# A graph layer with a mixture of experts on one core: the last loads of the expert outputs as two halves, their sums and stores in six pieces

## The reference

```python
xn = _layernorm(x, axis=-1)
x = x + _L0_gnn_ref(xn, edge_index, edge_attr_64, ...) + _L0_mix_ref(xn[None], ...)[0]
x = x + _L0_ffn_ref(_layernorm(x, axis=-1)[None], ...)[0]
...
    rw, re = jax.lax.top_k(probs, TOP_K)          # TOP_K = 2, weights made to sum to 1
    out = tokens
    for e in range(E):
        h = jax.nn.gelu(tokens @ w1[e] + b1[e], approximate=False)
        y = h @ w2[e] + b2[e]
        out = out + combine[:, e:e + 1] * y
```

## Time and profile before

| | us |
|---|---|
| median of 3 runs | 1223.35 (1216.89 to 1226.21) |
| profiled execution, own time | 1224.02 |
| profiled execution, span of the core | 1222.2 |
| last scatter of expert outputs issued (GpSimd) | 1181.99 |
| first load of the tail issued | 1184.14 |
| VectorE's last add ends | 1217.39 |

### The profile page before, as it was taken

How to read it: one execution, slowest core, us unless ns; L and a number is a source line. 1 busy time by engine, 2 the same in 40 slices (tenths; PEclk the granted TensorE clock), 3 DMA queues, 4 the chain that set the end, 5 groups by cost and what they waited for, 6 DMA issues and landing times.

```text
span 1222.2 us, 20643 instructions
## 1 busy us (share of the span) xinstructions
PE 943.8 (77%) x6706; PEld 678.6 (56%) x6707; DVE 677.0 (55%) x2018; ACT 357.3 (29%) x912; POOL 781.7 (64%) x575
## 2 busy tenths in 40 slices
PE   2308998798778999999999999925997008999960
PEld 2304544344336888888887888814886005666630
DVE  2306998677576666666566666305878402333324
ACT  0082232122113434434443444402434002222210
POOL 2588888888888888788888888860016771333320
PEclk9999999988898999999999999967979558999985
DMA  9944555545444565565555554467223232222239
GB/s 332 224 56 44 106 91 102 80 41 108 75 39 66 91 101 86 79 109 92 83 91 92 92 84 41 40 113 231 75 69 99 77 92 74 87 87 84 86 93 261
DMA packets 152487, 121.43 MB, mean 99 GB/s; under 512 B 123015, under 2 KB 142035, under 8 KB 148435
## 3 DMA queue, kind: packets, MB, share of 16 engines
q0 software_dynamic: 69376, 31.04, 24.8%
q1 hardware_dynamic: 76098, 75.82, 22.2%
q10 hardware_dynamic: 6926, 13.44, 3.5%
HBM read 75.23 MB, written 45.88 MB: 99 GB/s over the span
## 4 chain that ended last, share of the span: by engine, by line
PE 57%; POOL 17%; DMA 9%; issue 6%; DVE 5%; ACT 3%; SPq 1%; ACTq 0%; POOLq 0%; DVEq 0%
POOL edge_sums L636 14%; PE ps L1198 8%; PE ps L1043 7%; PE ps L1015 7%; PE ps L908 6%; PE ps L952 4%; PE ps L938 3%; PE ps L1024 3%; POOL routed_rows L659 3%; DMA edges<-in_edge_attr 3%; PE ps L1142 3%; DMA r2t<-expert_outputs 2%; PE ps L1199 2%; DMA edge_sums<-sums,addr 2%; PE ps L1047 2%
## 5 line engine op out<-in xcount | busy, mean ns | idle before, releaser
L636 POOL DMA_INDIRECT edge_sums<-sums,addr x416 | 648.0, 1558 | 159.9 <-issue 120.9
L908 PE MATMUL ps<-edges,same 128*128 128x65 f32 x832 | 121.2, 294 | 59.4 <-DMA edges<-in_edge_attr 36.2
L791 ACT ACTIVATE r<-ps 128x500 f32<-128x500 f32 (+1 forms) x225 | 126.2, 586 | 114.4 <-PE ps L1015 81.3
L908 PEld LDWEIGHTS ps<-edges,same 128*128 128x128 f32 x832 | 109.1, 206 | 79.9 <-DMA edges<-in_edge_attr 36.1
L1271 DVE SCALAR_TENSOR_TENSOR same<-srow,src_f,below 128x128 f32<-128x128 int32 x416 | 118.3, 346 | 39.2 <-DMA srow<-in_src_row 38.9
L667 POOL DMA_INDIRECT expert_outputs<-r x56 | 54.4, 972 | 120.9 <-DVE r L1648 118.3
L701 ACT ACTIVATE sums<-ps 128x260 f32<-128x260 f32 x104 | 40.7, 392 | 269.3 <-PE ps L908 172.0
L1198 PE MATMUL ps<-r2t,r 128*128 x448 | 117.6, 385 | 0.3 <-issue 0.3
L1381 DVE TENSOR_TENSOR r2t<-ps,r 125x2048 f32<-125x2048 f32 x50 | 113.1, 2262 | 0.0
L1015 PE MATMUL ps<-ident,r2t 125*128 125x125 f32 x800 | 105.8, 275 | 3.8 <-DVE r2t L1381 3.3
L1043 PE MATMUL ps<-r 128*64 128x125 f32 x1600 | 108.2, 277 | 0.0
(11 more groups left out here) (224 smaller groups left out, 1351.0 us busy)
## 6 DMA issues: line engine op xcount, KB each, us to landing
srow<-in_src_row SPq DMA_DIRECT2D x26, 1024.0 KB, 5.4
edges<-in_edge_attr SPq DMA_DIRECT2D x26, 512.0 KB
r<-routed_rows SPq DMA_DIRECT2D x56, 129.0 KB, 2.0
edge_sums<-sums,addr POOLq DMA_INDIRECT x416, 3.3
hpre_rows<-r ACTq DMA_DIRECT2D x25, 250.0 KB, 2.8
r<-hpre_rows SPq DMA_DIRECT2D x25, 250.0 KB, 2.7
edge_sums<-sums SPq DMA_DIRECT2D x4, 1040.0 KB, 14.6
r2t<-in_ew SPq DMA_DIRECT2D x4, 1024.0 KB, 14.6
```

The source lines that it names most:

```text
L636: pool.indirect_dma_start(out=tables[k], out_offset=bass.IndirectOffsetOnAxis(ap=addr[:, j:j + 1], axis=0), in_=sums[:, j % OR, :], in_off ...
L791: act.activation(phT[0:rows, j // 2 % 2 * 2 + j % 2, :], bank(1 + j % 2, rows, 0, QC * P), ACT.Copy).then_inc(grp_ready[j % 2], 1)
L908: m = mm(bank(b, 128, c0 + k * F, c0 + (k + 1) * F), lhsT=same[:, j % SR, :], rhs=edges[:, h, j % CH, :], start=True, stop=True)
```

## The change

Instead of five groups of 5 tiles, the loads come in two halves, of 13 tiles (into `r2t`) and 12 tiles (into `r1`, the large work buffer whose expert tiles are free by then). Each load now takes 13312 or 12288 bytes per partition in one run, and there are 8 load DMAs in place of 20. The sums and the stores are in six pieces of 5, 4, 4 tiles (first half) and 4, 4, 4 (second half). Pieces 0, 2, 4 are stored from SP, pieces 1, 3, 5 from ACT: 12 store DMAs in place of 10. The bytes loaded, added and stored are the same.

```diff
+        HALVES = ((0, 13), (13, T))
+        PIECES = ((0, 5), (5, 9), (9, 13), (13, 17), (17, 21), (21, T))
...
         def outputs_of(g):
-            if g < 2:
-                at_ = (srow[:, :, :].rearrange("p h c -> p (h c)").bitcast(fp32), sums[:, :, :].rearrange("p r f -> p (r f)"))[g]
-                return at_[0:P, 0:2 * FT * C].rearrange("p (a t c) -> p a t c", a=2, t=FT)
-            w = 2 * FT * C
-            return r2t[0:P, (g - 2) * w:(g - 1) * w].rearrange("p (a t c) -> p a t c", a=2, t=FT)
+            t0, t1 = HALVES[g]
+            at_ = (r2t, r1)[g][0:P, 0:2 * (t1 - t0) * C]
+            return at_.rearrange("p (a t c) -> p a t c", a=2, t=t1 - t0)
...
-            for g in range(T // FT):
+            for g, (t0, t1) in enumerate(HALVES):
                 for a, z in PARTS:
                     sp.dma_start(outputs_of(g)[a:z, 0, :, :], youts[0:N, :]
-                                 .rearrange("(p t) c -> p t c", p=P)[a:z, g * FT:(g + 1) * FT, :]).then_inc(yb_loaded[g], 16)
-            for g in range(0, T // FT, 2):
-                sp.wait_ge(yb_added, g + 1)
+                                 .rearrange("(p t) c -> p t c", p=P)[a:z, t0:t1, :]).then_inc(yb_loaded[g], 16)
+            for i, (t0, t1) in list(enumerate(PIECES))[0::2]:
+                sp.wait_ge(yb_added, i + 1)
                 for a, z in PARTS:
-                    sp.dma_start(out.rearrange("(p t) c -> p t c", p=P)[a:z, g * FT:(g + 1) * FT, :],
-                                 x_res[a:z, g * FT:(g + 1) * FT, :]).then_inc(stored, 16)
-            sp.wait_ge(stored, 32 * (T // FT))
+                    sp.dma_start(out.rearrange("(p t) c -> p t c", p=P)[a:z, t0:t1, :], x_res[a:z, t0:t1, :]).then_inc(stored, 16)
+            sp.wait_ge(stored, 32 * len(PIECES))
...
             v.wait_ge(res_ready, T)
-            for g in range(T // FT):
-                xv = x_res[:, g * FT:(g + 1) * FT, :]
+            for t0, t1 in PIECES:
+                g = t0 // HALVES[1][0]
+                lo = t0 - HALVES[g][0]
+                xv = x_res[:, t0:t1, :]
                 v.wait_ge(yb_loaded[g], 64)
-                link(v.tensor_tensor(xv, xv, outputs_of(g)[:, 0, :, :], ALU.add))
-                v.tensor_tensor(xv, xv, outputs_of(g)[:, 1, :, :], ALU.add).then_inc(yb_added, 1)
+                link(v.tensor_tensor(xv, xv, outputs_of(g)[:, 0, lo:lo + t1 - t0, :], ALU.add))
+                v.tensor_tensor(xv, xv, outputs_of(g)[:, 1, lo:lo + t1 - t0, :], ALU.add).then_inc(yb_added, 1)
```

More of the change, by code:

```diff
@@ L366, in gps_layer @@
         ys_stored = [sem(f"ys_stored{h}") for h in range(SB)]
-        yb_loaded = [sem(f"yb_loaded{g}") for g in range(T // FT)]
+        yb_loaded = [sem(f"yb_loaded{g}") for g in range(len(HALVES))]
         yb_added = sem("yb_added")
@@ L884, in _ @@
             act.wait_ge(ey_ps, NS)
-            for g in range(T // FT):
+            for g, (t0, t1) in enumerate(HALVES):
                 for a, z in PARTS:
                     act.dma_start(outputs_of(g)[a:z, 1, :, :], youts[N:2 * N, :]
-                                 .rearrange("(p t) c -> p t c", p=P)[a:z, g * FT:(g + 1) * FT, :]).then_inc(yb_loaded[g], 16)
-            for g in range(1, T // FT, 2):
-                act.wait_ge(yb_added, g + 1)
+                                  .rearrange("(p t) c -> p t c", p=P)[a:z, t0:t1, :]).then_inc(yb_loaded[g], 16)
+            for i, (t0, t1) in list(enumerate(PIECES))[1::2]:
+                act.wait_ge(yb_added, i + 1)
                 for a, z in PARTS:
-                    act.dma_start(out.rearrange("(p t) c -> p t c", p=P)[a:z, g * FT:(g + 1) * FT, :],
-                                 x_res[a:z, g * FT:(g + 1) * FT, :]).then_inc(stored, 16)
+                    act.dma_start(out.rearrange("(p t) c -> p t c", p=P)[a:z, t0:t1, :], x_res[a:z, t0:t1, :]).then_inc(stored, 16)
         @block.tensor
```

## The result

The changed kernel takes 1225.84 us in the median of 20 runs (1219.06 to 1232.02), the kernel before 1219.32 in 20 (1212.71 to 1227.88). The ratio is 1.0041 with a 95% interval of 1.0022 to 1.0061: 2.7 to 7.4 us slower, 5.0 in the middle. (The means, 1225.3 and 1220.2, lie 5.1 us apart, the medians 6.5.) The profiled execution has a span of 1224.7 us.

What follows compares the result with a forecast made beforehand. The prediction took the 38.1 us tail to be bound by transfers: loads, last adds, last store. Its terms, -1.85 - 0.9 + 4.5 - 0.9 = +0.85 us on a median of 1223.35, gave 1224.2 us, range 1217 to 1230.

Steps and rivals of the forecast that it cites:

- rival B: Tail: the loads gain nothing and the sums cost all, +3.6 us, 1227.0 us; chance 0.25.
- Fewer groups: Tail loads: one dip in the rate between two halves instead of four between five groups, -1.85 us.
- Longer rows: Tail loads: rows of 13312 bytes in one run raise the rate from 269 to 280 GB/s, -0.9 us.
- The loads' end: Landing of the last load: 1211.6 us instead of 1214.38, with bounds of 1210.0 and 1215.8.
- The adds of the second half: VectorE behind the last load: six adds take 7.5 us where two took 3.0, +4.5 us.
- The last store: End of the tail: 3.9 us from last add to end instead of 4.8, bounds 3.5 and 4.8, -0.9 us.
- Hidden parts: First half's sums (1199.2 to 1207.3) end before the second half lands, their stores wait behind the loads: nothing on the path.
- rival C: Tail: stores of pieces 0 to 2 run among the loads and delay the second half, +5.35 us, 1228.7; chance 0.05.
- rival D: Tail loads: rows are cut into pieces of about today's size, only the dips go, +1.75 us, 1225.1; chance 0.10.
- A store waits for all loads ahead of it: DMA queues of the tail: each takes its DMAs in order, so stores do not run among the loads.
- Rival A: Tail loads: long rows run at full rate, 384 GB/s, -4.9 us, 1218.4 us; chance 0.12.

Runs made afterwards that it cites:

- no13: The changed kernel without the loads of partitions 112 to 124; its loads took 24.5 us, against 31.0 and 31.7 with all rows.
- before_no13: The kernel before, five groups kept, without the loads of partitions 112 to 124; its loads took 24.3 us.
- spread13: The changed kernel with the rows of partitions 112 to 124 loaded into partitions 0, 9, 18 .. 108 of free places instead; loads took 27.5 us.
- wide_before: The kernel before with its five groups, each load one DMA over 128 partitions; ratio to before 0.9934, tail 29.0 us.

## Why the prediction was right or wrong

**The verdict** was right: no change beyond 1% either way, and 1225.84 lies in 1217 to 1230. The sign of the forecast's +0.85 us was too, its size was not: 5.0 were measured. That 1225.84 lies so near the forecast 1224.2 is luck. Its base, the median of three runs, was 4.0 us above the 1219.32 of 20, and its change about 4 us too small; the two errors cancel. In outcome it is rival B, named with a chance of 0.25: the loads gain nothing and the sums cost all, 3.6 us there and 4.7 in the tails here. B's reason, a lag of one engine behind another that is taken once, is not what the runs show.

**Fewer groups, -1.85 us: the step that failed.** It read that each dip stands at a group's end and put its price on the end. The alternative stood beside it: the dip belongs to the bytes. The rows of before could not tell the two apart, as all five groups had equal bytes. no13 and before_no13 show the owner, the DMA of partitions 112 to 124; spread13 shows the reason, the place it writes to; and the dip of 5, 13 and 20 tiles grows with their bytes. One dip of 2.5 us stands where four cost 2.5 together: nothing was saved in place of 1.85. The sentence from the Trainium skill on the semaphore's write fitted the dips and was not their cause: before_no13 kept five groups and their semaphores and had none.

**Longer rows, -0.9: wrong.** The flat stretches stayed at 263 and 278 GB/s, and without the 13 rows both kernels needed 24.3 to 24.5 us. I had taken the 303 GB/s near `x_res` as a sign for long rows. It holds other traffic, and its share of 1.17 should have weighed more. What the two loads of the earlier trace rows differ in was in the code: that of `x_res` goes through `PARTS`, 112 + 13 partitions (L494), and the expert weights at 384 GB/s go to 128 (L523), with the shorter rows.

**The loads' end: 1.8 us later in the means, not 2.75 earlier.** Counted from the first issue of before, the landing in after is at 1215.2, just past the 1215 that the prediction had named as a sign of being wrong. The part that grew is after the last flat stretch. With five groups a dip falls on rows of 5 tiles at the very end; with halves on rows of 12, and nothing more is to be loaded beside them. That this is the whole of the 1.8 us is argued, not shown.

**The adds of the second half: +4.5 forecast, +4.3 measured.** An add of 1024 took 1.22 to 1.23 us, as worked out from 1280 and 1625. The 0.2 is in the gaps (below).

**The last store: -0.9 forecast, -1.3 and -1.4 measured,** 3.5 us, the lower bound. SP's whole last wait of 4.8 us starts earlier, as its own last store does not end the tail any more.

**Hidden parts: right.** The first half's adds began 18.7 us after the first issue, 3.6 later than the forecast's 15.1 (1199.2 less 1184.14), and were still through 4.6 us before the second half landed. Until 1207 no store moved (rival C): in 1200 to 1207 of after, both queues moved alike, with SP's store of piece 0 issued at 1204.57 and ACT's of piece 1 at 1206.97:

```profile
q1 hardware_dynamic: 79, 0.97, 51.2%
q10 hardware_dynamic: 78, 0.96, 50.3%
```

79 packets for 0.97 MB are rows of 12 to 13 KB, so the loads are taken in one run, and rival D falls too. After 1207 stores did start; their packets are the ones of 2 to 8 KB, 15 of them in 1207 to 1209 (33 less 18):

```profile
DMA packets 72, 0.55 MB, mean 275 GB/s; under 512 B 18, under 2 KB 18, under 8 KB 33
```

and 73 more in 1209 to 1212, while the second half landed at 1213.90. The prediction had named stores before 1209 as a sign of being wrong. "A store waits for all loads ahead of it" was too strong: it does so until the last rows of its queue are under way. What the stores cost the end of the loads no run shows; as some 1.0 MB ran beside it in both kernels, it need not differ between them.

**Rival A** (loads at 384 GB/s, 1218.4 us) had the right suspicion that 269 GB/s was no limit of the DMA engines, and the wrong lever. The rate it asked for, and more, came with 128 partitions and not with longer rows. The figure of the Trainium skill that stood with it (341 GB/s for 1 MB) was not reached by loads of 1.5 MB over 112 partitions. The rule of the Trainium skill to use 128 partitions per DMA ("DMA: Bandwidth & Descriptors", Rules for kernel authors) is the one that this kernel breaks. The runs agree with it: keeping it was worth 8.5 us of tail in the kernel before and 11.7 in the changed one (means of the first table against the last one).

## What to carry to other kernels

Where a load's rate lies well below what the same engines reach elsewhere in the trace, ask which partitions it writes, before asking how long its rows are: here 112 + 13 partitions gave 269 GB/s with dips, and 128, three of them with rows that nobody reads, gave 412 to 430. When the groups of a pipeline are made larger, the work behind the last one grows with them; count it at full price and ask for proof of what is to pay for it. A price read off equal groups (per group, or per byte?) is two hypotheses, and the range should hold both.

## What the runs showed of the hardware

- A DMA of 13 rows into neighbouring partitions holds up both load queues: 37 GB/s in the worst microsecond, with a DMA share of 1.46 just before. Without it, or with its rows in scattered partitions, no slice there was under 197. Turning round the order on one queue moved that time and saved none.
- Stores read the same 112 + 13 partitions and suffered less: 367 GB/s in before, 317 in wide_before.
- The add that opens a new piece starts 0.09 us before the end of the one ahead, where no wait stands between them; the second add of a piece, which needs the first one's result, starts 0.03 us after its end. In the timeline of after, the add from 1215.16 takes 1.23 us and the next starts at 1216.30; the chain shows it as a piece of 1.15 us.
